# Attention scores from two float32r parts in halves of the PE rows, in place of three bfloat16 parts

## The reference, cut to what matters

```
x = x + 0.5 * ffn(layernorm(x))          # top-1 of 8 experts, D 128, hidden 512
x = x + attention(layernorm(x))
x = x + 0.5 * ffn(layernorm(x))

def attention(x):                        # x is (4, 1024, 128), float32
    q, k, v = heads(x @ Wq + bq), heads(x @ Wk + bk), heads(x @ Wv + bv)   # 16 heads of 8
    scores = einsum('bhsd,bhtd->bhst', q, k) * 8 ** -0.5
    ctx = einsum('bhst,bhtd->bhsd', softmax(scores), v)
    return merge(ctx) @ Wo + bo
```

## Time and profile before

| | us |
|---|---|
| median of 3 runs | 1001.35 |
| lowest and highest run | 998.92 and 1003.1 |
| span of the profiled execution | 996.9 |

### The profile page before, as it was taken

One profiled execution on the slowest core, in us unless ns is written; L12 is line 12 of the kernel. 1 busy time (PEld: TensorE's weight loads), 2 busy tenths in 40 slices (PEclk: granted clock), 3 DMA queues, 4 the chain that ended last, 5 costly groups with the idle time before them and its releaser, 6 DMA issues. The chain is left out here.

```text
span 996.9 us, 18005 instructions
## 1 busy us (share of the span) xinstructions
PE 907.5 (91%) x5949; PEld 385.6 (39%) x6023; DVE 832.2 (83%) x1404; ACT 750.2 (75%) x1507; POOL 219.1 (22%) x317
## 2 busy tenths in 40 slices
PE   5799927899999999999999999999999999965996
PEld 4699923322222222222222222222222222434996
DVE  6776628989999999999999999999999998768664
ACT  4367706978888888888888888888888888754774
POOL 3168841831000000000000100000100000024775
PEclk9989957999999999999999999999999999996998
DMA  7632135752220213202022120220202000051311
GB/s 262 194 96 73 41 116 190 238 192 63 58 61 16 62 34 81 62 17 62 15 73 74 31 62 15 73 54 28 75 30 64 29 23 17 2 169 48 105 63 44
DMA packets 65443, 75.14 MB, mean 75 GB/s; under 512 B 12896, under 2 KB 43784, under 8 KB 65352
## 3 DMA queue, kind: packets, MB, share of 16 engines
q1 hardware_dynamic: 58776, 60.98, 20.6%
q0 software_dynamic: 5120, 12.59, 4.1%
q10 hardware_dynamic: 1456, 0.41, 0.2%
HBM read 40.47 MB, written 33.49 MB: 74 GB/s over the span
## 5 line engine op out<-in xcount | busy, mean ns | idle before, releaser
L1574 DVE TENSOR_REDUCE maxima<-ps_m 128x2 f32<-128x1024 f32 x512 | 602.8, 1221 | 53.8 <-PE ps_m L1335 52.8
L1544 ACT ACTIVATE probs<-ps_s 128x512 f32<-128x512 f32 x1024 | 555.9, 600 | 109.5 <-PE ps_s L1381 77.7
L1381 PE MATMUL ps_s<-q,k 74*128 74x512 bf16 (+1 forms) x950 | 294.5, 385 | 3.0 <-ACT probs L1544 0.9
L1392 PE MATMUL ps_o<-probs,vs 128*32 128x512 f32 x2048 | 272.7, 605 | 0.7 <-ACT probs L1544 0.7
L1381 PEld LDWEIGHTS ps_s<-q,k 74*128 74x128 bf16 (+1 forms) x1024 | 79.5, 97 | 303.4 <-ACT probs L1544 217.1
L1335 PE MATMUL ps_m<-k,q 64*128 64x512 bf16 x1024 | 159.9, 385 | 13.8 <-ACT probs L1544 7.9
L1265 POOL TENSOR_SCALAR split<-top 128x16 bf16<-128x16 f32 x32 | 8.1, 253 | 445.8 <-DVE top L1590 428.7
L1335 PEld LDWEIGHTS ps_m<-k,q 64*128 64x128 bf16 x1024 | 49.1, 93 | 102.7 <-issue 58.1
L693 PE MATMUL ps_y<-W,hT 128*128 x624 | 83.8, 278 | 0.0
L1392 PEld LDWEIGHTS ps_o<-probs,vs 128*32 128x32 f32 x2048 | 40.3, 108 | 109.3 <-issue 95.1
L693 PEld LDWEIGHTS ps_y<-W,hT 128*128 128x128 f32 x624 | 77.0, 194 | 0.6 <-issue 0.4
(11 more groups left out here) (215 smaller groups left out, 586.3 us busy)
## 6 DMA issues: line engine op xcount, KB each, us to landing
k_rows<-parts SPq DMA_DIRECT2D x24, 384.0 KB, 4.5
sums<-oT SPq DMA_DIRECT2D x30, 256.0 KB, 3.6
q<-q_parts SPq DMA_DIRECT2D x75, 96.0 KB
k<-k_rows SPq DMA_DIRECT2D x15, 288.0 KB
token_rows<-x SPq DMA_DIRECT2D x16, 256.0 KB, 4.1
token_rows<-v_and_ctx SPq DMA_DIRECT2D x16, 256.0 KB, 3.6
k<-k_rows SPq DMA_DIRECT2D x15, 256.0 KB
q_parts<-parts SPq DMA_DIRECT2D x8, 384.0 KB, 3.4
```

The source lines that it names most:

```text
L1381: nc.tensor.matmul(ps_s[n % 3][:, :], k2[buffer(g)][0:contracted, j, kt * P:(kt + 1) * P], q2[buffer(g)][0:contracted, j, u * HALF:(u + 1) ...
L1392: last = nc.tensor.matmul(ps_o[32 * j:32 * (j + 1), :], vs[buffer(g)][:, kt, j, :], probs[:, s % 2, j, :], start=(kt == 0), stop=(kt == KT ...
L1544: nc.scalar.activation(probs[:, s % 2, j, :], ps_s[n % 3][:, :], ACT.Exp, scale=SCALE).then_inc(exped, 1)
L1574: nc.vector.tensor_reduce(maxima[:, :, pr, qt, kh], ps_m[slot][:, :, :], AX.X, ALU.max).then_inc(unit_free[slot], 1)
```

## The change

Queries and keys are carried as two float32r parts (ACT, DVE and POOL write them rounded to float32r, each in 4 bytes). 2 x 2 pairs of parts times 8 dimensions make 32 rows a head. Head j (even) has rows 0 to 63, head j + 1 rows 64 to 127; row 32 is a zero row of q against ones of k, rows 33 and 34 are the guards. Maxima contract 33 rows, scores 35, each in its own half of PE's rows. The order of matmuls within a step stays. The second rounding on ACT (16 instructions) and the third part (10 on POOL, 6 on DVE) are gone. Stores are two a quad in place of four; a group's load is 12 DMAs in place of 10. SPLITS is 2. There are 5 fill pieces a buffer. The diff, cut to its core:

```diff
-PARTS = 3
+PARTS = 2
 ROWS = PARTS * PARTS * DK
-MAX_ROWS = ROWS - DK
+ODD = P // 2
 GUARDS = 2
-SCORED = ROWS + GUARDS
+GUARD = ROWS + 1
+SCORED = GUARD + GUARDS
-SPLITS = 3
+SPLITS = 2
...
-    FILLED = 4 * BUFS
+    PIECES = 5
+    FILLED = PIECES * BUFS
     def gpsimd_fill(self, pool, n):
-        p, piece = n // 4, n % 4
+        p, piece = n // self.PIECES, n % self.PIECES
         if n:
             pool.wait_ge(self.filled, n)
-        if piece == 0:
-            self.nc.gpsimd.memset(self.k2[p][64:96, 0::2, :].bitcast(F32), self.PAIR).then_inc(self.filled, 1)
...
+        if piece < 2:
+            self.nc.gpsimd.memset(self.k2[p][piece * ODD + ROWS:piece * ODD + SCORED, :, :].bitcast(F32), 1.0).then_inc(self.filled, 1)
+        elif piece < 4:
+            start = (piece - 2) * ODD + ROWS
+            self.nc.gpsimd.memset(self.q2[p][start:start + 1, :, :].bitcast(F32), 0.0).then_inc(self.filled, 1)
+        else:
             self.nc.gpsimd.memset(self.vs[p][:, :, :, :], 1.0).then_inc(self.filled, 1)
...
-        q2, k2 = ([sb(f"{n}{p}", [P, GH, SEQ], BF16) for p in range(BUFS)] for n in ("q2_", "k2_"))
+        q2, k2 = ([sb(f"{n}{p}", [P, GH // 2, SEQ], F32R) for p in range(BUFS)] for n in ("q2_", "k2_"))
...
-                    for j in (2 * pr, 2 * pr + 1):
-                        rows = slice(j % 2 * MAX_ROWS, (j % 2 + 1) * MAX_ROWS)
-                        last = nc.tensor.matmul(ps_m[slot][:, j % 2, :], q2[buffer(g)][rows, j, qt * P:(qt + 1) * P],
-                                                k2[buffer(g)][rows, j, kh * HALF:(kh + 1) * HALF], start=True, stop=True)
+                    for j in range(2):
+                        rows = slice(j * ODD, j * ODD + GUARD)
+                        last = nc.tensor.matmul(ps_m[slot][:, j, :], q2[buffer(g)][rows, pr, qt * P:(qt + 1) * P],
+                                                k2[buffer(g)][rows, pr, kh * HALF:(kh + 1) * HALF], start=True, stop=True)
...
-                    u, kt, n, contracted = k // KT, k % KT, GH * (STEPS * g + k) + j, (P if j % 2 else SCORED)
+                    u, kt, n, rows = k // KT, k % KT, GH * (STEPS * g + k) + j, slice(j % 2 * ODD, j % 2 * ODD + SCORED)
-                    nc.tensor.matmul(ps_s[n % 3][:, :], k2[buffer(g)][0:contracted, j, kt * P:(kt + 1) * P],
-                                     q2[buffer(g)][0:contracted, j, u * HALF:(u + 1) * HALF], start=True, stop=True).then_inc(scored, 1)
+                    nc.tensor.matmul(ps_s[n % 3][:, :], k2[buffer(g)][rows, j // 2, kt * P:(kt + 1) * P],
+                                     q2[buffer(g)][rows, j // 2, u * HALF:(u + 1) * HALF], start=True, stop=True).then_inc(scored, 1)
...
         def remainders(pool, q):
-            p = q % 2
-            if q >= 2:
-                parts_done(pool, low, q - 2, 2)
             for j in range(2):
                 pool.wait_ge(high, high_parts(q) + 2 * j + 2)
-                nc.gpsimd.tensor_tensor(rem[:, p, j, :], exact[:, p, j, :], parts[:, q % SPLITS, j, 0, :], ALU.subtract).then_inc(left[min(q, FIRST)], 1)
+                nc.gpsimd.tensor_tensor(parts[:, q % SPLITS, j, 1, :].bitcast(F32R), exact[:, q % 2, j, :], parts[:, q % SPLITS, j, 0, :], ALU.subtract).then_inc(left[min(q, FIRST)], 1)
...
                 load(1)
                 store(QUADS - 4)
-                store_key(sp, QUADS - 3, 0)
                 place_guard(0)
-                store_rest(QUADS - 3)
-                for q in range(QUADS - 2, QUADS):
+                for q in range(QUADS - 3, QUADS):
                     store(q)
```

More of the change, by code:

```diff
@@ L6 @@
 BF16 = mybir.dt.bfloat16
+F32R = mybir.dt.float32r
 I32 = mybir.dt.int32
@@ L972, in attention @@
         shift, primed = sb("shift_a", [P, TILES], F32), sb("primed", [P, 1], F32)
[L973 to L974 removed]
+        parts = sb("parts", [P, SPLITS, 2, PARTS, HALF], F32)
+        parts_flat = parts[:, :, :, :, :].rearrange("p a j m c -> p (a j m c)").bitcast(BF16)
         ctxT = ctx_sb[:, :, :, :].rearrange("p g t c -> p (g t c)")
@@ L982, in attention @@
         top, negated = (sb(name, [P, 2, GH // 2 * QUAD], F32) for name in ("top", "negated"))
-        split = sb("split", [P, 2, GUARDS, GH // 2 * QUAD], BF16)
-        blocks = [sb(f"blocks{p}", [P, 4 * KT], BF16) for p in range(2)]
+        split = sb("split", [P, 2, GUARDS, GH // 2 * QUAD], F32)
+        blocks = [sb(f"blocks{p}", [P, 4 * KT], F32) for p in range(2)]
         ps_m = [ctx.enter_context(nc.psum_tensor(f"ps_m{p}", [P, 2, HALF], F32)) for p in range(2)]
@@ L1012, in use, with product @@
             return g // BUFS
[L1014 to L1020, removed]
+        def product(j, n):
+            return j % 2 * ODD + n * PARTS * DK
         def load_queries(engine, g, landed, tokens=slice(0, SEQ)):
@@ L1036, in load_keys @@
             for j in range(2):
[L1037 to L1040, removed]
+                k_rows = dram["k_parts"][b, :, :, slice(first + j, first + GH, 2), tokens]
+                for n in range(PARTS):
+                    for m in range(PARTS):
+                        row = product(j, n) + m * DK
+                        engine.dma_start(k[row:row + DK, :, tokens].bitcast(F32), k_rows[n, :, :, :]).then_inc(landed, 16)
         def high_parts(q):
@@ L1053, in store_query, with store_key @@
             b, tokens = where(q)
-            parts_done(engine, low, q, 1)
+            parts_done(engine, q, 1)
             engine.dma_start(dram["q_parts"][b, :, :, :, tokens].rearrange("m d h t -> (d h) m t"),
                              parts[:, q % SPLITS, 0, :, :]).then_inc(query_stored if q < FIRST else parts_stored[q % SPLITS], 16)
-        def store_key(engine, q, n):
+        def store_key(engine, q):
             b, tokens = where(q)
[L1061 to L1068, removed]
+            parts_done(engine, q, 2)
+            engine.dma_start(dram["k_parts"][b, :, :, :, tokens].rearrange("m d h t -> (d h) m t"),
+                             parts[:, q % SPLITS, 1, :, :]).then_inc(parts_stored[q % SPLITS], 16)
         def stores_landed(engine, q):
@@ L1491, in high_part @@
                         nc.scalar.activation(exact[:, q % 2, j, :], bank[:, :], ACT.Identity, bias=bias[:, 0:1]).then_inc(high, 1)
-                    nc.scalar.activation(parts[:, q % SPLITS, j, 0, :], bank[:, :], ACT.Identity, bias=bias[:, 0:1]).then_inc(high, 1)
+                    nc.scalar.activation(parts[:, q % SPLITS, j, 0, :].bitcast(F32R), bank[:, :], ACT.Identity, bias=bias[:, 0:1]).then_inc(high, 1)
                 def high_both(q):
-                    parts_done(act, left, q - 2, 2)
+                    parts_done(act, q - 2, 2)
                     if q >= SPLITS:
@@ L1500, in high_both @@
                         high_part(q, j)
-                def second_part(q, j):
-                    parts_done(act, left, q, j + 1)
-                    nc.scalar.activation(parts[:, q % SPLITS, j, 1, :], rem[:, q % 2, j, :], ACT.Copy).then_inc(middle, 1)
                 front.scalar(act)
@@ L1532, in _ @@
                         normalise(q + 2)
-                    for j in range(2):
-                        second_part(q, j)
-                parts_done(act, low, LAST - 1, 2)
-                parts_done(act, low, LAST, 2)
+                parts_done(act, LAST - 1, 2)
                 for s in range(SOFT):
@@ L1684, in remainder @@
                     dve.wait_ge(high, high_parts(q) + j + 1)
-                    nc.vector.scalar_tensor_tensor(out=rem[:, q % 2, j, :], in0=bank[:, :], scalar=bias[:, 0:1], in1=parts[:, q % SPLITS, j, 0, :],
-                                                   op0=ALU.add, op1=ALU.subtract).then_inc(left[q % LAST], 1)
+                    nc.vector.scalar_tensor_tensor(out=parts[:, q % SPLITS, j, 1, :].bitcast(F32R), in0=bank[:, :], scalar=bias[:, 0:1],
+                                                   in1=parts[:, q % SPLITS, j, 0, :], op0=ALU.add, op1=ALU.subtract).then_inc(left[q % LAST], 1)
                 front.vector(dve)
@@ L1718, in _ @@
                             values(late.pop(0))
-                parts_done(dve, low, LAST - 2, 2)
                 for j in range(2):
@@ L1723, in _ @@
                     values(late.pop(0))
-                for j in range(2):
-                    third_part(dve, nc.vector, LAST, j)
                 for s, units in enumerate(SCHEDULE):
@@ L1814 @@
     dram["x_rows"] = nc.dram_tensor("x_rows", [TOKENS, D], F32).ap()
-    dram["guards"] = nc.dram_tensor("guards", [2 * GROUPS, 4 * KT, P], BF16).ap()
+    dram["guards"] = nc.dram_tensor("guards", [2 * GROUPS, 4 * KT, P], F32).ap()
     dram["sums"] = nc.dram_tensor("sums", [2, GROUPS, P, HALF], F32).ap()
     dram["inverse"] = nc.dram_tensor("inverse", [SPARSE, HEADS, HALF], F32).ap()
-    dram["q_parts"] = nc.dram_tensor("q_parts", [BATCH, PARTS, DK, HEADS, SEQ], BF16).ap()
-    dram["k_rows"] = nc.dram_tensor("k_rows", [BATCH, PARTS, PARTS, DK, HEADS, SEQ], BF16).ap()
+    for name in ("q_parts", "k_parts"):
```

(1 more changed line is left out.)

52 lines of the change are left out of this document (13 added, 39 removed).

## The result

The changed kernel takes 1395.83 us (median of 4 runs, 1391.05 to 1396.21), the kernel before 1000.3 us in runs beside it: a ratio of 1.393 (95% interval 1.390 to 1.396). The forecast was 991, the range 964 to 1006. It is wrong, in sign and in size.

A forecast was written before the change was run, and what follows sets the result against it. It took a loop over two steps through DVE's reductions and PE to bound the steps, with PE close beside; -24.5 (steps), +13.2 (fills) and +0.5 (prologue) make -10.8 us from 1001.35, forecast 991, range 964 to 1006.

The forecast's parts named there:

- A granted clock of 1.2 GHz: Sign of being wrong: PE's granted clock at 1.2 GHz in the steps; given no chance.
- 1. *Stream: PE matmuls: a float32r stream of 512 columns costs 0.22 us, as in bfloat16.
- slower, by the stream: Rival, PE streams: float32r costs more than 0.22; at 0.43 a step is 3.05, total 1120; chance 0.12.
- the pairs don't run beside each other: Rival, PE: each pair of 4-byte matmuls costs two streams, 2.85 a step, total 1071; chance 0.06.
- 2. *Weights: PE weight loads: 4-byte, 128 columns cost 0.11 us in the open, twice in the loop: second unit and score 3.
- 3. *Loop: Steps: the loop over two steps through DVE's reductions and their slot takes 5.03 us, so 2.515 a step.
- the rival's 2.42: Rival, PE weights load fast: the exposures fall away, 2.42 us a step, total 966; chance 0.12.
- 4. *Guards: Guard loads in the steps: 0.005 us a step added, giving 2.52 (bounds 2.48 and 2.56), term -24.5 us.
- 5. *Fills: POOL memsets among the scatters cost by columns, 1.87 us for 2048, adding 13.2 us on the path.
- The rival of cheap narrow memsets: Rival, POOL fills: memsets on few partitions are cheap, 10.7 us less, total 980; chance 0.08.
- 6. *Prologue: Before the steps: ACT's first part of quad 7 waits for quad 5's stores; +0.5 us, bounds -2 and +5.
- 7. *Steps 245 to 255: Last steps, without units: pairing's saving offset by shape changes and open weights; term 0, bounds -2 and +2.

The follow-up runs named there:

- e11_pad_middle: Changed kernel with rows 35 to 63 filled, scores contracting 64 rows in steps 96 to 127 only, 35 elsewhere: 1162.86 us.
- e1_pad: Changed kernel with guards moved to rows 62 and 63 and rows 32 to 61 filled, maxima on 62 rows, scores on 64: 1064.49 us, ratio 1.009.
- e6: e1_pad with the exponential of head 3 handling 256 of 512 queries from step 2 on: median step 2.545 us.
- e7: e1_pad with DVE's reduction of a step's second unit reading 384 of 512 keys a head: step 2.607 us.
- e3: Kernel before, still bfloat16, with maxima contracting 33 rows and scores 35: 1093.09 us, 1.037 of the kernel before.
- e2: Changed kernel with quad 5's stores issued before the first guards are placed: 1438.07 us, 1.364 of the kernel before.
- e9: e1_pad with whole-tile fills (nine) moved ahead of POOL's gathers and quad 5's stores before the guards: 990.41 us, 0.990 of the kernel before.
- e10: Kernel before, with only its twelve fills moved from among the scatters to ahead of POOL's gathers: 988.36 us, ratio 0.988.
- e8_pad_first: Changed kernel with rows 32 to 63 filled, scores contracting 64 rows in steps 0 to 31, then 35, maxima on 33: 1057.02 us, ratio 1.009.
- e4_pad_scores: Like e1_pad, but only the scores contract 64 rows and the maxima stay at 33: 1064.09 us.

## Why the prediction was wrong

The step that failed stands in the first paragraph of its reading, "PE is busy 614 of 625 us at the full clock". It was carried over without a term to an array with nearly half of its rows empty, and every duration of points 1 to 4 was a full-clock one. The runs showed 1.2 GHz and 4.07 us a step in its place, against 2.52 forecast. A granted clock of 1.2 GHz stood among the signs of being wrong, but had no chance and no price among the rivals. Its price could have been had from the rows: PE's parts doubled are 2 x 2.08 = 4.16 us a step, which is more than the loop, so 245 x (4.16 - 2.62) = 377, and 14 for points 5 and 6, on 1001: 1392. Measured were 4.07 and 1396. No row of before could show that it would happen, since all its streams stand on 64 rows or more; that was a reason to give it a chance.

The Trainium skill (TensorE: Matmul & The Clock Gate, Part 1: The HAM clock gate) has the clock follow how busy the engine has been. This case's traces do not agree as far as a busy record goes: PE's records fill 950 us of 950 at 0.50, and 360 of 360 in e11_pad_middle, and there the clock is up 3.2 us after the first score on more rows, with PE as busy as before.

Point by point:

1. *Stream*: right. One pass, 0.43 at 1.2 GHz; in e1_pad at 2.4 GHz scores 0 and 1 start together, and where its weights are not in the open the next stream starts 0.23 to 0.27 later. The 0.43 that was named as a sign of being wrong did appear, but from the clock. The rivals "slower, by the stream" and "the pairs don't run beside each other" are false as mechanisms.
2. *Weights*: right in size, 0.11 in the open (score 3 to the unit's second matmul is 0.33), but in three places, not two: score 3, the second unit and score 2.
3. *Loop*: at full clock 2.61 and not 2.515. The term that was mis-sized is the 2.19 from the second unit to the next one: 2.36, and the 0.17 more all lie at score 2, whose bank frees late. The loop of a score bank through exp had not been looked for; e6 and e7 (one run each) show that it binds. The PE time that the change saves is spent waiting for it. Fast weights would have given 2.46 (e3), not the rival's 2.42.
4. *Guards*: small, as said; the mean step of e1_pad is 2.62 against a median of 2.61. By the mean, the change saves next to nothing a step even at the full clock (2.626 in the kernel before).
5. *Fills*: right as a cost. 1.80 us each (1.87 said), on 1, 3, 30, 32 and 128 partitions alike; +12.5 us (13.2 said), x at 152.75 (153 to 154 said). The rival of cheap narrow memsets is false. That they lie on the path was true only of their place among the scatters.
6. *Prologue*: the mechanism was right, ACT's first part of quad 7 behind quad 5's store; the size was not: +3.6 us from the x load to the first step where +0.5 was taken, within its bounds. The order of e2 gives it back: in e9 the first step comes 188.16 - 130.28 = 57.9 us after the x load, before it was 61.0.
7. *Steps 245 to 255*: 3.17 us for a step with an output projection in e9_fills_early (values at 857.26 and 860.43), 2.86 in the kernel before (868.91 and 871.77). Over the last steps, from the values of step 243 to the last, e9 takes 35.3 us and e10 32.8: it loses 2.5, outside the +2 that was the bound. That every change to the 4-byte streams opens weights would make it so, but no run tests it. After the last values e9 takes 2.4 us more than e10; why is open.

The main case's own range, 977 to 1005, is a little narrower than its bounds add up to (976 to 1007).

With the clock kept, the change comes to this (e9 less e10, spans 988.3 and 986.3): x load +0.5, prologue -2.9, first steps at the low clock +1.3, the others up to 243 -0.0076 x 238 = -1.8, last steps +2.5, after them +2.4, in all 2.0. It is level within what can be told. That e9 lands at the forecast 991 is chance: its steps give 2 us where 24.5 were forecast, and its fills give 10 where 13 were to be lost.

## What to carry to other kernels

Before the rows that a matmul contracts are cut, look whether the clock stands high and what will lift it again if it falls; padding to 64 rows cost no PE time here (a step of 2.61 on 64 rows in e1_pad and on 35 in e8_pad_first) and brought 2.4 GHz back, and padding the scores of the first 32 steps alone was enough. Saved PE time counts only against every loop through a buffer: follow each PSUM bank through its reader, not just the one with the busiest engine. And work that must be done sometime belongs in an engine's long wait, which moved more time here (10 us) than the whole change did at equal clock.

## What the runs showed of the hardware

- The granted clock depends on the height of the matmuls, not only on how full PE's record is: with 33 and 35 rows PE, busy 100%, stayed at 1.2 GHz for 1036 us; 64 rows in the scores alone lifted it, 3.2 us after the first of them in e11_pad_middle (614.60 to 617.8) and 6.6 and 16.7 us after the first step in e8_pad_first and e4_pad_scores; and 585 us of narrow steps after that did not lower it (e8_pad_first). In bfloat16 it came back by itself after 232 us (e3_bf16_few); why is open, and so is what lets it fall at the end of the prologue, which it did in every kernel here but the one before and e10_before_fills.
- A float32r matmul passes 512 columns once, and two on separate halves of the rows run beside each other as in bfloat16; its 128 columns of weights cost 0.11 us wherever they cannot load behind a stream (0.333 us to the next start where a hidden load gives 0.23, e1_pad).
- A wait for a buffer stands on the weight load, so with 4-byte weights a late buffer costs the wait and the load: score 2 to values is 0.43 us in e1_pad and 0.31 before.
- A POOL memset costs by its columns: 2048 take 1.80 us on 1 partition (changed kernel) and 1.81 on 128 (e9_fills_early).
